# Two edge layers of a graph network: GpSimd's gathers of table rows are tied to TensorE's one-hot gathers

## The chip, the cores and the metric

The kernel runs on one core of one Trainium2 chip. The metric is the device time of that core in microseconds. The kernel before took 4427.94 us, the median of three runs that lie between 4411.06 and 4448.39 us.

## The reference

The network has 6250 nodes with 16 features and 206250 edges, sorted by their destination. Four layers follow each other, each as `x = x + layer(relu(layernorm(x)))`. The first (six graph convolutions) and the third (one) are done as dense products with an adjacency matrix. The change touches only the second and the fourth, whose messages hang on each edge's own type:

```
# second layer, 8 edge types
A     = edge_emb[edge_type_8].reshape(-1, 16, 16)
msg   = einsum('emh,eh->em', A, h[src])
m     = segment_sum(msg, dst, 6250)          # then a GRU step of m and h
# fourth layer, 90 edge types
e     = concat([h[src] @ Ws.T, edge_attr @ Ws.T, h[dst] @ Ws.T]) @ Wa.T
msg   = einsum('ei,eio->eo', h[src], W_rel[edge_type_90]) * e
h_out = segment_sum(msg, dst, 6250)
```

## The kernel before, in words

The edges are padded to 206848 and cut into 202 **supertiles** of 1024 edges (8 columns of 128 edges). Both edge layers go through the supertiles in one loop each, and each supertile is done in one of two ways.

- **By matmul** ("one-hot supertiles"). SyncE loads the source keys of the 1024 edges, VectorE compares them with `at_key` and writes one-hot matrices (`make_hot`, L1818 in the second layer, L2195 in the fourth), TensorE multiplies the node table with them (`gather`, 24 matmuls at L1832 and 4 at L1828, or 28 at L2214), ScalarE evicts the result in four pieces (L1838, L2220), TensorE folds it (L1848, L2229), and the messages are made and summed by destination. The fourth layer also expands the relation weights with 24 matmuls (L2249) and multiplies on VectorE (L2277, L2269).
- **By table.** A table of all products (node, type) was written to HBM before (`typed_table`). GpSimd fetches each edge's finished row with an indirect DMA, 8 of them for a supertile, one for 128 edges (`fetch_rows`, L1809; `fetch_table_rows`, L2180). TensorE sums the rows by destination (`row_sums`, L1915; `add_up`, L2301).

In the second layer (`typed_layer`) 122 supertiles go by matmul (list `PK`) and 80 by table (list `GK`). In the fourth (`relation_layer`) list `EK` holds 106: the first 11 are "plain" (GpSimd fetches rows of h, L2166, while TensorE still builds the table, L2133), 95 go by matmul, and 96 go by table (`GK`). `after[i]` lists the table supertiles that lie behind the i-th entry of PK or EK. It holds one or none in the second layer, and one nearly always in the fourth, where three places hold two: i = 43, 74 and 105, the last.

The loop is software-pipelined and written out by hand. Turn i issues, in this order on the engines: the key loads of a later supertile (SP), the table fetches of `after[i]` (POOL), the fold of supertile i-1 (PE, ACT), the destination one-hots and one-hots for i+1 (DVE), the gather of supertile i (PE), and the sums of older ones, among them the table supertiles of `after[i-3]` (second layer) or `after[i-2]` (fourth). Between engines only semaphores order the work. GpSimd's queue holds nothing but its fetches in these loops, so it runs ahead of the turn that issues them until it finds no free buffer: `fetch_rows(g)` waits for the sums of table supertile g-8 (`a_tok[g - RG]`, RG = 8), `fetch_table_rows(g)` for those of g-12 (RT = 12). The first fetch of each layer waits for the table's last stores. The token `gat[i, HALVES - 1]` is given by TensorE's last matmul of the gather of supertile i; ScalarE and VectorE wait for it too.

After each edge layer there is a barrier of all engines.

Of the kernel before, what the change touches and what calls it, by code (L numbers as in the profile page):

```python
# [55 lines left out]
HALVES = 2  # L56
# [64 lines left out]
def program(nc, t, wcols, out):  # L121
    pe, dve, act, pool, sp = nc.tensor, nc.vector, nc.scalar, nc.gpsimd, nc.sync
# [1156 lines left out]
    def layers_fast(h_tok):  # L1279
# [414 lines left out]
        def typed_layer(x_spread, HT):  # L1694
# [6 lines left out]
            after = [[g for g, k in enumerate(GK) if PK[i] < k and (i + 1 == n or k < PK[i + 1])] for i in range(n)]  # L1701
# [37 lines left out]
            keys_tok, hot_tok, gat, selt, fold_tok, G_tok, typed_tok, byt_tok, bytc_tok, m_tok, a_tok, dst_tok, r_tok_, sum_tok, out_tok = ({} for _ in range(15))  # L1739
# [52 lines left out]
            def load_keys(i):  # L1792
                b = i % 3
                if i >= 3:
                    sp.wait_ge(*hot_tok[i - 3])
                e = slice(PK[i] * SE, (PK[i] + 1) * SE)
                k_in[b].by(sp.dma_start(krow[b][:, :], key2_dram[:, e].to_broadcast([P, SE])), 16)
                rows8 = last_dram[2 * PK[i]:2 * PK[i] + 2].rearrange("h r e -> (h r) e").rearrange("r (q e) -> r q e", q=1)
                keys_tok[i] = k_in[b].by(sp.dma_start(klast[b][:, :], rows8.to_broadcast([8, LASTK, HE])), 16)
# [157 lines left out]
            for i in range(n + 3):  # L1957
                if i + 2 < n:
                    load_keys(i + 2)
                if i == n:  # L1960
                    sp.wait_ge(*hot_tok[n - 1])
                    sp.wait_ge(*gat[n - 1, HALVES - 1])
                    load_place(RING, passes.order[::-1][RING])
                if i < n:
                    for g in after[i]:
                        fetch_rows(g)
                if 1 <= i <= n:
                    fold_rows(i - 1)
                    keep_rows(i - 1)
                if i >= 2 and i - 2 < n:  # L1970
                    for g in after[i - 2]:
                        make_dst(g)
                if i + 1 < n:
                    make_hot(i + 1)
                if 1 <= i <= n:
                    make_typed(i - 1)
                if i < n:
                    gather(i)
                if i >= 2:
                    sum_types(i - 2)  # L1980
                if 2 <= i <= n + 1:
                    keep_types(i - 2)
                if i >= 3:
                    keep_sums(PK[i - 3], m_tok[i - 3], i - 3)
                    store_sums(PK[i - 3], i - 3)
                    for g in after[i - 3]:
                        row_sums(g)
                        keep_sums(GK[g], a_tok[g])
                        store_sums(GK[g])
# [42 lines left out]
        def relation_layer(x_spread, terms, wx, w_ready):  # L2032
# [23 lines left out]
            after = [[g for g, k in enumerate(GK) if EK[i] < k and (i + 1 == n or k < EK[i + 1])] for i in range(n)]  # L2056
            by_matmul = [kinds[k] == "matmul" for k in EK]
# [30 lines left out]
            keys_tok, hot_tok, ty_tok, gat, selt, fold_tok, G_tok, w_tok, prod_tok, e_tok, msg_tok, a_tok, sum_tok = ({} for _ in range(13))  # L2088
# [240 lines left out]
            for i in range(n + 2):  # L2329
                tiles = range(min(NT, TILES[i]), min(NT, TILES[i + 1])) if i < PLAIN else ()  # L2330
                if i + 1 < n:
                    load_edges(i + 1)
                if i < n:
                    for g in after[i]:
                        fetch_table_rows(g)
                ahead = 1 if 1 <= i < PLAIN else len(tiles)
# [176 lines left out]
```

## Time and profile before

| what | value |
|---|---|
| median of three runs | 4427.94 us (4411.06 to 4448.39) |
| profiled execution, span from first to last instruction | 4521.8 us |
| mean granted TensorE clock in it | 0.868 |
| PE busy | 3700.8 us (82%) |
| DVE busy | 2709.2 us (60%) |
| POOL busy | 1876.4 us (41%) |
| ACT busy | 1320.5 us (29%) |
| loop of the second layer | about 1478 to 2733 us of the span |
| loop of the fourth layer | about 2950 to 4504 us, by matmul and table from about 3059 us |

The profile shows one execution. For that execution no time besides its span is given, and the span is 93.9 us longer than the median of the timed runs. An engine's share counts its instructions alone, not its waits. A matmul's end is modelled in the profile, so that the moment at which another engine is released by it tells more of TensorE's real progress than the matmul rows do. "issue" as the end of idle time means that the profile shows nothing for which the engine waited; "remote" that the semaphore's giver could not be named. The granted clock is a share of 2.4 GHz: 1.00 is 2.4 GHz, 0.50 is 1.2 GHz, and other values are means over a stretch.

### The profile page before, as it was taken

The page shows a single profiled execution, that of the slowest core. Times are in us where ns is not written, and L with a number is a line of the kernel's source. Part 1 is how long each engine was busy: PE and PEld are TensorE (multiplying, and loading weights), DVE is VectorE, ACT ScalarE, POOL GpSimd, SP SyncE. Part 2 cuts the span into 40 slices and gives each one's busy share as a digit, 9 for nine tenths or more (in the row PEclk, how much of TensorE's full clock was granted, in tenths as well). Part 3 has the DMA queues.
Part 4 walks back from the last instruction along what each step waited for, and adds up shares of the span by engine and source line. Part 5 has one row for each costly group of instructions (what it writes and reads, how often), then busy time and mean ns, then how long its engine had stood idle before and what let it go on. Part 6 is the DMA issues. An engine that isn't in the chain of part 4 may idle for free. (4 is left out here: it accounts for less than half of the span.)

```text
span 4521.8 us, 77858 instructions
## 1 busy us (share of the span) xinstructions
PE 3700.8 (82%) x28548; PEld 2135.0 (47%) x28548; DVE 2709.2 (60%) x6415; ACT 1320.5 (29%) x2874; POOL 1876.4 (41%) x1856
## 2 busy tenths in 40 slices
PE   6778869999997488897888795482799988998898
PEld 4666635544554143443444443241455555555555
DVE  8999933222213265666666574252577777776778
ACT  7899910011000122332332231150122212221222
POOL 1000058400000545666666540437366565655550
PEclk8999979999997688898899897665788889888888
DMA  5444477533447111221122126671122221221111
GB/s 143 80 80 80 80 316 286 213 150 153 162 184 295 45 44 41 51 51 45 46 49 49 41 51 200 216 261 34 31 47 43 43 41 39 47 41 40 42 40 42
DMA packets 471197, 445.63 MB, mean 99 GB/s; under 512 B 357554, under 2 KB 406610, under 8 KB 459676
## 3 DMA queue, kind: packets, MB, share of 16 engines
q1 hardware_dynamic: 389178, 391.82, 27.6%
q0 software_dynamic: 55216, 38.70, 5.1%
q10 hardware_dynamic: 26417, 10.05, 0.9%
q8 instruction: 232, 3.80, 0.3%
q14 instruction: 154, 1.25, 0.1%
HBM read 346.18 MB, written 95.85 MB: 98 GB/s over the span
## 5 line engine op out<-in xcount | busy, mean ns | idle before, releaser
L1809 POOL DMA_INDIRECT rows<-typed_table,ring x640 | 734.7, 1148 | 472.0 <-PE ps_x L1915 263.5
L2214 PE MATMUL l_ps_g<-ring,h_part 128*128 128x512 f16 x2660 | 656.3, 406 | 142.8 <-issue 101.5
L1409 PE MATMUL L_ps<-ring,L_T 128*128 128x448 fp8e4 (+1 forms) x4606 | 678.3, 394 | 68.6 <-DMA ring<-adj 54.2
L2180 POOL DMA_INDIRECT ring<-typed_table,l_idxA x384 | 397.9, 1036 | 349.7 <-PE l_ps_x L2301 192.5
L1409 PEld LDWEIGHTS L_ps<-ring,L_T 128*128 128x128 f16 (+1 forms) x4606 | 329.6, 107 | 403.9 <-issue 70.0
L2214 PEld LDWEIGHTS l_ps_g<-ring,h_part 128*128 128x128 f16 x2660 | 275.0, 104 | 492.6 <-issue 202.3
L2180 POOL DMA_INDIRECT l_rows<-typed_table,l_idxA x384 | 393.8, 1025 | 248.5 <-PE l_ps_x L2301 144.0
L2220 ACT ACTIVATE l_sel<-l_ps_g 128x512 f16<-128x512 f32 x380 | 225.4, 597 | 900.6 <-PE l_ps_g L2214 373.9
L619 PE MATMUL cells<-keys,lows 128*128 128x147 f16 (+5 forms) x2744 | 373.1, 283 | 119.5 <-DVE keys L580 104.0
L1838 ACT ACTIVATE sel<-ps_g 128x512 f16<-128x512 f32 x488 | 264.1, 595 | 537.4 <-PE ps_g L1832 314.0
L2195 DVE TENSOR_SCALAR ring<-l_krow,W 128x1024 f16<-128x1024 f16 x570 | 234.7, 482 | 301.0 <-remote 164.9
L2249 PE MATMUL l_ps_w<-rel,l_tyh 90*128 90x256 bf16 x2544 | 400.1, 328 | 17.1 <-DVE ring L2277 12.1
L1832 PE MATMUL ps_g<-dinvB,h_part 128*128 128x512 f16 x1464 | 383.2, 422 | 27.9 <-issue 27.8
L619 PEld LDWEIGHTS cells<-keys,lows 128*128 128x128 f16 x2744 | 286.8, 141 | 203.1 <-DVE keys L580 170.7
L1868 DVE TENSOR_TENSOR dinvB<-G,tyh 128x1024 f16<-128x1024 f16 x244 | 288.2, 1222 | 135.3 <-issue 87.4
L1421 DVE SCALAR_TENSOR_TENSOR L_Y<-L_ps,L_scale,dinvB 128x448 f32<-128x448 f32 x84 | 57.4, 683 | 520.3 <-PE L_ps L1409 520.2
L580 DVE TENSOR_SCALAR keys<-build_or_wx,offset 128x441 f16<-128x441 f16 (+3 forms) x1438 | 366.3, 329 | 0.0
L1832 PE MATMUL ps_g<-ring_fifth,h_part 128*128 128x512 f16 x1464 | 349.8, 394 | 11.3 <-issue 10.7
L2249 PEld LDWEIGHTS l_ps_w<-rel,l_tyh 90*128 90x128 bf16 x2544 | 287.9, 116 | 99.4 <-issue 27.2
L697 ACT ACTIVATE ring<-cells 128x784 fp8e4<-128x784 f32 x392 | 325.1, 830 | 24.7 <-PE cells L619 24.4
L2277 DVE TENSOR_TENSOR ring<-l_ps_w,l_G 128x512 f32<-128x512 f32 x380 | 258.6, 683 | 85.2 <-remote 71.3
L2269 DVE TENSOR_REDUCE l_msg<-ring 128x32 f32<-128x512 f32 x424 | 277.6, 676 | 0.0
(369 smaller groups left out, 4468.1 us busy)
## 6 DMA issues: line engine op xcount, KB each, us to landing
ring<-adj SPq DMA_DIRECT2D x67, 2744.0 KB, 10.3
adj<-ring SPq DMA_DIRECT2D x14, 2744.0 KB, 9.1
typed_table<-ring SPq DMA_DIRECT2D x49, 765.0 KB
ring_fifth<-src_div_mod_rows SPq DMA_DIRECT2D x122, 256.0 KB
l_krow<-src_div_mod_rows SPq DMA_DIRECT2D x95, 256.0 KB
l_trow<-type_row SPq DMA_DIRECT2D x106, 180.0 KB
attr<-in_he POOLq DMA_DIRECT2D x25, 512.0 KB, 8.1
klast<-last_keys SPq DMA_DIRECT2D x81, 128.0 KB
```

Source lines behind the costliest of these rows:

```text
L580: ins = dve.tensor_scalar(keys[g % OB][:, j, 0:C], iotaC[:, 0:C], offset[g // BG % 2][:, g % BG, j:j + 1], HIT, ALU.is_equal, ALU.mult)
L619: ins = pe.matmul(to, lows[g // QG % 3][:, :, g % QG * KT + j], made[:, (a1 - a) * NT:(b1 - a) * NT], start=j == FIRST[h], stop=j == LAST[ ...
L697: act.activation(ring[c % RING][:, :, gl * GD:(gl + 1) * GD].rearrange("p k (h d) -> p k h d", h=2), cells[g % CB][:, :, 0:HD * NT].rearra ...
L1409: ins = pe.matmul(bank[at:at + rows, 0:CH], d["T"][q][:, k, 0:rows], ring[r][:, k, :], start=n < side, stop=n >= NT - side, tile_position= ...
L1809: r_tok_[g] = r_in[b].by(pool.indirect_dma_start(rows[b][:, j, :], None, t1_dram, bass.IndirectOffsetOnAxis(ap=idxA[:, k * SUP + j:k * SUP ...
L1832: ins = pe.matmul(ps_g[2 * h + p][:, 0:HE], parts[p][:, j, :], hot[b][:, j, h * HE:(h + 1) * HE], start=False, stop=j == GJ - 2)
L1838: selt[i, h] = c_sel.by(act.activation(sel[b][2 * h + p][:, :], ps_g[2 * h + p][:, 0:HE], ACT.Relu))
L1868: typed_tok[i] = c_typed.by(dve.tensor_tensor(typed[b][:, p, :, :, :], gp, ty, ALU.mult))
L2180: rt_tok[g] = r_in[b].by(pool.indirect_dma_start(table_rows[b][:, j, 0:RC], None, t3_dram, bass.IndirectOffsetOnAxis(ap=idxA[:, k * SUP + ...
L2214: ins = pe.matmul(ps_g[p][:, 0:HE], parts[p][:, j, :], hot[b][:, j, h * HE:(h + 1) * HE], start=j == 0, stop=j == GJ - 1)
L2249: ins = pe.matmul(ps_w[q][:, (j % 2) * 256:(j % 2 + 1) * 256], tyh[i % 3][:, j * P:(j + 1) * P], rel[:, p, :], start=p == 0, stop=p == 2)
L2269: return c_msg.by(dve.tensor_reduce(m[:, 2 * q:2 * q + 2, 0:F], prod[q], AX.X, ALU.add))
```

## The change

Before the fetches of turn i, GpSimd now waits until TensorE has finished the gather of supertile i-2, in both layers. In the fourth layer the wait is left out where supertile i-2 is a plain one. Nothing else changes: no buffer, no size, no other wait.

```
@@ -1962,6 +1962,8 @@        (typed_layer)
                     sp.wait_ge(*gat[n - 1, HALVES - 1])
                     load_place(RING, passes.order[::-1][RING])
                 if i < n:
+                    if i >= 2 and after[i]:
+                        pool.wait_ge(*gat[i - 2, HALVES - 1])
                     for g in after[i]:
                         fetch_rows(g)
                 if 1 <= i <= n:
@@ -2331,6 +2333,8 @@        (relation_layer)
                 if i + 1 < n:
                     load_edges(i + 1)
                 if i < n:
+                    if i >= 2 and after[i] and by_matmul[i - 2]:
+                        pool.wait_ge(*gat[i - 2, HALVES - 1])
                     for g in after[i]:
                         fetch_table_rows(g)
                 ahead = 1 if 1 <= i < PLAIN else len(tiles)
```

## Rows read from the trace of the kernel before

**Rows 1.** The page, engines: busy time, share of the span, instructions.
```profile
PE 3700.8 (82%) x28548; PEld 2135.0 (47%) x28548; DVE 2709.2 (60%) x6415; ACT 1320.5 (29%) x2874; POOL 1876.4 (41%) x1856
```

**Rows 2.** Windows, fourth layer, L2180 alone: us, POOL busy (count), clock, DMA, GB/s.
```profile
3059.00:3183.00 124.00, 94.10 (x96) 0.54 0.12 19
3183.00:3232.00 49.00, 0.00 (x0) 0.81 0.12 32
```

**Rows 3.** Windows, fourth layer: us, busy of PE, PEld, DVE, ACT, POOL; clock, DMA, GB/s.
```profile
3078.00:3196.00 118.00, 21.29 (x88) 6.96 (x86) 11.08 (x25) 2.01 (x5) 79.08 (x84) 0.53 0.09 11
3196.00:3232.00 36.00, 35.21 (x266) 21.45 (x266) 30.95 (x72) 9.38 (x21) 0.00 (x0) 0.87 0.16 43
...
3300.00:4300.00 1000.00, 902.20 (x7028) 554.59 (x7027) 735.90 (x1682) 211.98 (x491) 595.98 (x576) 0.87 0.21 42
...
4401.00:4490.00 89.00, 89.00 (x808) 57.58 (x805) 80.63 (x185) 24.87 (x57) 0.33 (x1) 1.00 0.11 31
```

**Rows 4.** Windows, fourth layer, L2220 alone, four evictions for each gather.
```profile
3078.00:3196.00 118.00, 1.54 (x3) 0.53 0.09 11
3196.00:3232.00 36.00, 7.90 (x14) 0.87 0.16 43
...
3300.00:4300.00 1000.00, 165.67 (x279) 0.87 0.21 42
...
4401.00:4490.00 89.00, 19.60 (x33) 1.00 0.11 31
```

**Rows 5.** Timeline of DVE in the fourth layer: start, us, instruction, idle before.
```profile
3115.89 0.69 DVE L2277 TENSOR_TENSOR ring<-l_ps_w,l_G 128x512 f32<-128x512 f32 x1 [21.62 <-remote]
...
3149.44 0.69 DVE L2277 TENSOR_TENSOR ring<-l_ps_w,l_G 128x512 f32<-128x512 f32 x1 [31.51 <-remote]
```

**Rows 6.** Timeline of PE in the second layer, while GpSimd gathers.
```profile
1550.99 0.58 PE L1832 MATMUL ps_g<-dinvB,h_part 128*128 128x512 f16 x1 [2.21 <-issue]
1553.79 0.58 PE L1832 MATMUL ps_g<-dinvB,h_part 128*128 128x512 f16 x1 [2.21 <-issue]
```

**Rows 7.** Windows, second layer, L1809 alone (columns as in rows 2).
```profile
1479.00:1563.00 84.00, 64.19 (x64) 0.62 0.11 21
1563.00:1605.00 42.00, 0.00 (x0) 0.87 0.15 39
...
1700.00:2660.00 960.00, 604.90 (x520) 0.89 0.21 47
```

**Rows 8.** Windows, second layer, L1838 alone, four evictions for each gather.
```profile
1485.00:1526.00 41.00, 4.56 (x9) 0.71 0.10 16
1526.00:1575.00 49.00, 2.28 (x5) 0.51 0.05 5
1575.00:1605.00 30.00, 9.29 (x18) 1.00 0.21 55
...
1700.00:2660.00 960.00, 209.99 (x388) 0.89 0.21 47
...
2677.00:2721.00 44.00, 12.92 (x25) 1.00 0.15 40
```

**Rows 9.** Timeline of DVE, second layer, one-hots of two turns running.
```profile
1582.09 2.46 DVE L1818 TENSOR_SCALAR ring_fifth<-ring_fifth,W 128x1024 f16<-128x1024 f16 x6 [1.49 <-PE ps_g L1832]
...
1589.44 2.46 DVE L1818 TENSOR_SCALAR dinvB<-ring_fifth,W 128x1024 f16<-128x1024 f16 x6 [0.89 <-PE ps_g L1832]
```

**Rows 10.** Timeline, fourth layer: last eviction of gather 23, first use of group 12.
```profile
3343.58 0.60 ACT L2220 ACTIVATE l_sel<-l_ps_g 128x512 f16<-128x512 f32 x1 [0.86 <-remote]
...
3381.19 0.29 DVE L2293 TENSOR_TENSOR ring<-ring,l_eG 128x128 f32<-128x128 f32 x1
```

**Rows 11.** Timeline, end of the second layer: evictions of gather 119, last row sums.
```profile
2706.04 1.08 ACT L1838 ACTIVATE sel<-ps_g 128x512 f16<-128x512 f32 x2 [1.50 <-PE ps_g L1832]
...
2727.98 1.04 PE L1915 MATMUL ps_x<-rows,dstw 128*64 128x16 f32 x16 [0.36 <-ACT sums L1926]
```

More of the change, by code:

```diff
@@ L1964, in typed_layer @@
                 if i < n:
+                    if i >= 2 and after[i]:
+                        pool.wait_ge(*gat[i - 2, HALVES - 1])
                     for g in after[i]:
@@ L2333, in relation_layer @@
                 if i < n:
+                    if i >= 2 and after[i] and by_matmul[i - 2]:
+                        pool.wait_ge(*gat[i - 2, HALVES - 1])
                     for g in after[i]:
```

## The prediction

> **What bounds the kernel now.** I read the engines' shares first. TensorE is busy 82% of the span, GpSimd 41% [rows 1], so no gather of GpSimd's should be on the path by its share. Then I laid windows over the two loops that the change touches, and beside each asked for GpSimd's gathers alone and for ScalarE's evictions alone. Four evictions make one TensorE gather, so their count is the speed at which the loop goes.
>
> In the fourth layer GpSimd may start once the table is stored. It then runs through all its twelve free buffers: 96 gathers in 124 us, and then it stands still for 49 us [rows 2]. Over the same time TensorE nearly stops. From 3078 to 3196 us there are 3 evictions, less than one gather, and the granted clock is 0.53; when the burst is over, 36 us see 14 evictions, 3.5 gathers, at 10.3 us each [rows 3, 4]. The steady part, where GpSimd gathers one group per turn, takes 1000 us for 279 evictions: 14.3 us a gather at a clock of 0.87. The last 89 us have no gather of GpSimd's, and 33 evictions: 10.8 us each at a clock of 1.00, with the same work on every other engine [rows 3, 4].
>
> The stall is TensorE's own. VectorE waits 21.6 and 31.5 us for the products of twelve matmuls each [rows 5]; the two releases are 33.6 us apart, 2.8 us for each matmul. In the second layer the matmul rows show that pace directly, one each 2.80 us with "issue" before it, so no semaphore of the profile holds it [rows 6]. There the burst is 64 gathers in 84 us [rows 7]; its gathers 1 to 3 take from 1485 to 1575 us (14 evictions, window edges included) and then 4.5 gathers take 30 us, where the one-hots of two turns start 7.35 us apart [rows 8, 9]. With GpSimd busy it is 960 us for 388 evictions, 9.90 us a gather; in the last 44 us without it, 25 evictions, 7.0 us [rows 8].
>
> So the profile says: while GpSimd gathers, TensorE is slower by 14.3 - 10.8 = 3.5 us a turn in the fourth layer and by 9.9 - 7.35 = 2.5 us in the second, and after some 20 us of unbroken gathering it falls to a crawl. Slower gathering with pauses costs TensorE far less than a burst.
>
> **The change, part by part.** The added waits are some 170 on a queue that holds nothing else in these loops; behind each stands only the group that it guards. Their own time is at most an ordinary step of that queue: the burst's 96 gathers take 1.28 us each with 0.98 us of it busy [rows 2], so 0 to 0.3 us, hidden, since GpSimd has idle time in every turn (596 us busy in 1000 [rows 3]).
>
> *The bursts go.* In the fourth layer groups 0 and 1 still start early (the first has no wait, the second one for gather 11, which is done before 3078), but group 2 waits for gather 12, group 3 for gather 13, and so on. The pace of the steady part should hold from there. From 3078 to 4490 us, 94 gathers take 1412 us now (the ends of the windows of [rows 4]). At 14.34 us (1000 x 4 / 279) they take 1348 us: **-64 us**. This already charges the ten groups that used to be fetched in the stall, and the end of the loop, now without gathers, at the full steady price.
>
> In the second layer the first group (behind entry 4 of PK) waits for gather 2. Gathers 1 and 2 then go at 7.35 us: 14.7 us instead of 41 (1485 to 1526 [rows 8]). The 119 gathers from 3 to 121 take 119 x 9.90 = 1178 us, instead of 1195 (1526 to 2721): together **-43 us**.
>
> The other way round: the stalls are worth 118 - 14.3 = 104 us and 90 - 22 = 68 us (three gathers at 7.35), and the gathers that move to where TensorE now runs alone cost, per turn, 3.5 us for 8.25 turns (29), 14.3 - 10.3 = 4 us for 3.5 turns (14), 9.9 - 7.0 = 2.9 us for 6.25 turns (18) and 9.9 - 6.7 = 3.2 us for 4.5 turns (14) [rows 4, 8]: 172 - 75 = 97 us. The two sums agree within 10 us. I take 107, since it uses the long steady windows.
>
> *Arrival of the rows.* A group was fetched up to twelve groups ahead and now starts when gather i-2 is done. In the fourth layer gather 23 is done at 3343.6 and the rows of turn 25 are first used at 3381.2 [rows 10], 37.6 us later. A group of eight takes 8 x 1.28 = 10.3 us, and two together, where `after` holds two, 20.6. That is hidden, with 17 us to spare. If that cover went, each such place would cost a few us, three times. The tightest place is the end of the second layer: group 79 may start at 2706.0, but groups 77 and 78 are before it (gates 14.7 and 7.35 us earlier, 8 x (604.9 / 520 + 0.3) = 11.7 us each), so it ends near 2691.3 + 3 x 11.7 = 2726.4, and TensorE wants it at 2728 [rows 7, 9, 11]. I set 0 us and keep 0 to 5 us for the range.
>
> *Where two rows and a rule differ.* Rows 3 and 6 show TensorE slow only while GpSimd gathers. That is also the sign that this is contention and not a wait. The Trainium skill (SBUF — State Buffer, section "Who interferes with whom") states the contrary: a DMA never contends with a compute engine, only VectorE and GpSimd share ports, and TensorE and ScalarE never wait on anyone. By that rule the bursts could not be what stalls TensorE, and the change would bring nothing from them.
>
> Sum: -107 us on a span of 4521.8, that is 4415. The timed median stands 94 us below that span, and I carry the difference over unscaled: 4427.9 - 107 = **4321 us**. What part of the slowdown is there without the profiler is the main unknown. Its bounds are 0 and all. The slowdown beside gathers that the windows hold is 172 us of stalls, 1000 / 14.3 x 3.5 = 245 us and 960 / 9.9 x 2.5 = 242 us [rows 4, 8], 659 us together. The timed runs are only 94 us shorter than the span, so most of it must be in them too. I stay near "all".
>
> **The rivals.** *Half.* TensorE starts to crawl soon after 3078 us, when GpSimd has gathered for only 19 us, and groups 0 and 1 (22 us) and the pairs of the second layer remain unbroken. If half of the stalls stays, 172 / 2 - 75 = 11 us are won: 4417.
>
> *Only in the profile.* The 94 us between span and runs are of the size of the stalls that would go. If the crawl belongs to the profiled execution, the timed runs don't change: about 4428. Against it speak the 659 us above. The Trainium skill (NOTIFIC — the notification-queue block, section 7.1) says that the path of the trace records can hold an engine back; no row here shows that path.
>
> *Slower.* The stall is not due to the burst but to the start of the loop (first keys, cold buffers), and happens anyway at the same place; then only the price of moved gathers is left, +75 us: 4503. It decides against the change from the point where less than 75 of the 172 us go away. For it: gathering and TensorE's work overlap more than before. Against it: the crawl ends 12 or 13 us after the burst in both layers (3183 and 3196, 1563 and 1575 [rows 2, 4, 7, 8]), at different places of their loops, and VectorE and ScalarE only wait in it. The rule above would favour this case or the one before.
>
> **How the numbers follow.** Forecast 0.60, half 0.10, only in the profile 0.17, slower 0.13. The forecast's own range is 4270 to 4375: lower if the steady part of the fourth layer becomes quicker too (0.5 us a turn makes 47), higher if a third of the stalls stays (+57). The range to 4440 takes in the rivals "half" and "only in the profile" and leaves out the slower one and the forecast's lower tail. 1% (44 us) is about what a measurement of this kernel can tell from no change. Faster by more: 0.61; within: 0.26; slower: 0.13.
>
> **What would show it.** In the changed kernel's profile: no window of 100 us with fewer than 20 evictions at L2220 or L1838; GpSimd's 96 and 64 gathers spread out, its idle time ended by the gather's matmuls (L2214, L1832) instead of the sums (L2301, L1915); a steady turn of 14.3 and 9.9 us in the whole loop, and the clock no longer 1.00 in the last 90 us; no wait of VectorE's for fetched rows before L2292, none of TensorE's before L1915. The prediction is wrong if the two stalls stay, if a steady turn becomes longer than 15 or 10.5 us, or if the span falls and the runs don't.

## The result

| | median of the runs | ratio to before |
|---|---|---|
| before | 4434.97 us (4411.06 to 4448.39, 4 runs) | |
| changed | 4517.26 us (4512.33 to 4557.44, 4 runs) | 1.0203 [1.0155, 1.0252] |

The ratios, here and below, leave disturbed runs out, so they aren't always those of the medians. The forecast was 4321 us and faster. The kernel is 2% slower, and the time lies outside the range. The profiled execution of the changed kernel is one of its timed runs: 4512.33 us, with a span of 4508.4 us. Against the profiled execution of before (span 4521.8 us) it is 13 us *shorter*, so the two traces by themselves don't show the loss. Why is part of the answer below.

The page, engines, to lay beside [rows 1]:

```profile
PE 3746.4 (83%) x28548; PEld 2133.2 (47%) x28548; DVE 2704.2 (60%) x6415; ACT 1319.3 (29%) x2874; POOL 1915.0 (42%) x1856
```

The same instructions, and TensorE is busy 46 us longer. The windows of GpSimd's gathers at the start of the fourth layer, which now begins near 3104 us (the line numbers there have moved by two, L2180 is L2182; columns as in [rows 2]):

```profile
3104.00:3228.00 124.00, 70.89 (x65) 0.88 0.24 48
3228.00:3277.00 49.00, 34.28 (x32) 0.90 0.28 49
```

The 96 gathers in 124 us have become 65, and the 49 us of standing still are gone. Now the evictions of the one-hot gathers in the fourth layer, L2222, four for each gather, the answer to [rows 4]:

```profile
3123.00:3241.00 118.00, 21.39 (x36) 0.93 0.24 45
3241.00:3277.00 36.00, 5.37 (x9) 0.86 0.30 49
3345.00:4345.00 1000.00, 163.28 (x276) 0.86 0.22 41
4387.00:4476.00 89.00, 13.62 (x23) 0.83 0.13 19
```

The first 118 us hold 36 evictions where there were 3, and the clock in them is 0.93, not 0.53: the stall is gone. The steady part has 276 instead of 279 evictions in 1000 us. The last 89 us hold 23 instead of 33, because GpSimd now gathers to the end. The second layer, L1838, the answer to [rows 8]:

```profile
1481.00:1522.00 41.00, 9.45 (x18) 0.92 0.12 24
1522.00:1571.00 49.00, 8.68 (x16) 0.82 0.20 46
...
1700.00:2660.00 960.00, 195.09 (x364) 0.84 0.20 44
2730.00:2775.00 45.00, 7.67 (x15) 0.77 0.12 24
```

Here too the stall at the start is gone (34 evictions in 90 us, before 14). But the steady part has slowed: 364 evictions in 960 us are 10.55 us a gather, before it was 388 and 9.90 us, and the clock has gone from 0.89 to 0.84. What released GpSimd (sum of the waits, times, longest), of the whole span:

```profile
POOL rows L1809 <- PE ps_g L1832: 375.5, 37, 31.0
POOL ring L2182 <- PE l_ps_g L2216: 196.8, 29, 60.5
...
POOL l_rows L2182 <- PE l_ps_g L2216: 119.2, 27, 13.2
```

So the change does what it says: TensorE's gathers of the one-hot tiles release GpSimd in both layers. Two of the prediction's own signs of being wrong came true: a steady turn of the second layer is longer than 10.5 us, and the span fell while the runs didn't.

### The profile page after: what moved, and what is told of

It reads as the page before. It is cut to its first block and busy times, and to the rows that moved or that the text cites. A ratio compares the mean times of both kernels' runs of the same rounds, so it can differ in the third digit from the quotient of the medians.

```text
span 4508.4 us, 78017 instructions
## 1 busy us (share of the span) xinstructions
PE 3746.4 (83%) x28548; PEld 2133.2 (47%) x28548; DVE 2704.2 (60%) x6415; ACT 1319.3 (29%) x2874; POOL 1915.0 (42%) x1856
## 5 line engine op out<-in xcount | busy, mean ns | idle before, releaser
L1809 POOL DMA_INDIRECT rows<-typed_table,ring x640 | 731.3, 1143 | 564.3 <-PE ps_g L1832 375.5
L2182 POOL DMA_INDIRECT ring<-typed_table,l_idxA x384 | 419.1, 1091 | 317.8 <-PE l_ps_g L2216 196.8
L2182 POOL DMA_INDIRECT l_rows<-typed_table,l_idxA x384 | 415.6, 1082 | 242.7 <-PE l_ps_g L2216 119.2
L1838 ACT ACTIVATE sel<-ps_g 128x512 f16<-128x512 f32 x488 | 262.5, 596 | 561.7 <-PE ps_g L1832 347.2
L2222 ACT ACTIVATE l_sel<-l_ps_g 128x512 f16<-128x512 f32 x380 | 224.9, 597 | 644.2 <-PE l_ps_g L2216 415.1
L1832 PE MATMUL ps_g<-ring_fifth,h_part 128*128 128x512 f16 x1464 | 400.5, 439 | 2.6 <-issue 2.2
L2251 PEld LDWEIGHTS l_ps_w<-rel,l_tyh 90*128 90x128 bf16 x2544 | 269.2, 111 | 169.4 <-issue 111.4
```

The costliest lines, as they stand in the source:

```text
L1809: r_tok_[g] = r_in[b].by(pool.indirect_dma_start(rows[b][:, j, :], None, t1_dram, bass.IndirectOffsetOnAxis(ap=idxA[:, k * SUP + j:k * SUP ...
L1832: ins = pe.matmul(ps_g[2 * h + p][:, 0:HE], parts[p][:, j, :], hot[b][:, j, h * HE:(h + 1) * HE], start=False, stop=j == GJ - 2)
L1838: selt[i, h] = c_sel.by(act.activation(sel[b][2 * h + p][:, :], ps_g[2 * h + p][:, 0:HE], ACT.Relu))
L2182: rt_tok[g] = r_in[b].by(pool.indirect_dma_start(table_rows[b][:, j, 0:RC], None, t3_dram, bass.IndirectOffsetOnAxis(ap=idxA[:, k * SUP + ...
L2251: ins = pe.matmul(ps_w[q][:, (j % 2) * 256:(j % 2 + 1) * 256], tyh[i % 3][:, j * P:(j + 1) * P], rel[:, p, :], start=p == 0, stop=p == 2)
```

## Experiments

Ten different kernels, the kernel before among them, ran 18 times under a name of their own in five sittings, each beside runs of the kernel before on the same chip. The kernel before itself took very different times in them: 4530 us in sitting A, 3792 in B, 4511 in C, 4442 in D and 4449 in E. A, C and D were one chip, B and E two others. "Slowed" below means that TensorE is slower while GpSimd gathers, as in the trace ahead of the prediction; that was so in A, C, D and E and not in B.

### Sitting A (before 4530 us): each layer's wait alone

`b0_before` is the kernel before, unchanged. `typed_only` and `relation_only` are one half of the change each:

```
typed_only      +  if i >= 2 and after[i]:                          (second layer)
                +      pool.wait_ge(*gat[i - 2, HALVES - 1])
relation_only   +  if i >= 2 and after[i] and by_matmul[i - 2]:     (fourth layer)
                +      pool.wait_ge(*gat[i - 2, HALVES - 1])
lag6            both, with i - 6 in place of i - 2
```

> The kernel before, unchanged, for a second trace of it. Theory 'the profiled execution was not a typical one': the timed runs of before (median 4435) are some 90 us shorter than the one traced, and 90 us is about what the stalls at the start of the two loops cost, so the new trace has a span near 4430 and at least one of the stalls (119 us before gather 12 of the fourth layer, 49 us before gather 3 of the second) is gone or much shorter. Theory 'the stalls are always there': the span is again near 4520 or, if it is 4430, the steady turns are shorter and the two stalls stand. Ratio to before 1.00.

Measured: 4532.71 us, ratio 1.0036 [0.9997, 1.0074].

> The wait in the second layer alone. In the changed kernel's trace a turn of that loop takes 10.7 us against 9.9 in the trace of before, with GpSimd's groups in unbroken pairs. Theory 'pairs': the slow-down of the second layer is the larger part of the 82 us, so this kernel takes 50 to 80 us more than before (4485 to 4515). Theory 'moved gathers': each layer pays for the groups that used to be fetched in a burst, 8 here and 10 to 11 there, so this kernel takes 30 to 40 us more than before (4465 to 4475).

Measured: 4545.0 us, ratio 1.0046 [0.9997, 1.0095].

> The wait in the fourth layer alone. Theory 'pairs' (most of the loss is in the second layer): 5 to 30 us more than before (4440 to 4465). Theory 'moved gathers': 40 to 50 us more (4475 to 4485). If the stall before gather 12 were in the typical run of before, this kernel would be 60 us faster.

Measured: 4450.39 us, ratio 0.987 [0.9789, 0.995].

> Both waits, but for gather i-6 instead of i-2 (in the fourth layer the wait then begins at turn 17, so that four groups run free). The burst is limited to about 4 groups, and GpSimd stays some 7 turns ahead instead of 3. Theory 'moved gathers': the loss goes with the number of groups that no longer come early, so about half of the 82 us remains: 4470 to 4480. Theory 'pairs' (it is the moment in the turn and the unbroken pair that count, and both are as with i-2): nearly the whole loss remains, 4500 to 4520.

Measured: 4597.6 us, ratio 1.0166 [1.0074, 1.0257].

What follows: the stalls are no peculiarity of the one execution that was given, since `b0_before` shows them too and its span (4553.6 us) is 4 us below its own time. The fourth layer's wait wins there, by the mechanism of the prediction and near its size: its loop is 70 us shorter than in `b0_before` (the forecast's term was 64). Both theories that were written down for `relation_only`, 5 to 30 and 40 to 50 us more than before, missed. The second layer's wait wins nothing, although it too takes its stall away. And waiting on an older gather (i - 6), which leaves GpSimd a lead of six turns, is not the cure: the second loop got longest of all, 1361.5 us.

### Sitting B (before 3792 us): a chip on which TensorE isn't slowed

`after_again` is the changed kernel. `slots4` caps the burst of the second layer in another way, by row sums and not by gathers; its fourth layer is that of before. `halves` splits a group's eight fetches over two turns. `half_gathers` is the kernel before with half of the second layer's fetches left out, so that half of these messages is missing; it also clears the row buffers once (not shown).

```
slots4        -  if g >= RG:                       +  if g >= 4:
              -      pool.wait_ge(*a_tok[g - RG])  +      pool.wait_ge(*a_tok[g - 4])
halves        -  for j in range(SUP):
              +  for j in range(half * SUP // 2, (half + 1) * SUP // 2):
              (fetch_rows(g, 0) after gather i-3, fetch_rows(g, 1) after gather i-2)
half_gathers  -  for j in range(SUP):              +  for j in range(SUP // 2):
```

> The changed kernel, unchanged, beside before on the chip of this job. In the traces so far the wait in the fourth layer shortens its loop from 1404-1428 to 1355-1362 us, and the wait in the second layer moves its loop from 1211-1252 to 1247-1294 us. Theory 'two opposite effects, and a chip-dependent remainder': the sum is near zero, ratio to before 0.99 to 1.01. Theory 'the loss is the change's own everywhere': ratio 1.015 to 1.025 again.

Measured: 3865.84 us, ratio 1.0193 [1.017, 1.0216].

> The kernel before, but in the second layer a group may only be fetched when the sums of group g-4, not g-8, are done; the fourth layer as before. So the start burst is 4 groups, and GpSimd is about as near to TensorE as with the added wait, but it is released at the row sums, as before, and not at the end of the gather. Theory 'amount' (what counts is how many groups run ahead): like the wait in the second layer alone, loop 1247 to 1294 us, turns of 10.4 to 10.7. Theory 'moment' (what counts is at which point of TensorE's turn a group begins): turns of 9.5 to 9.9 as before, loop 1200 to 1220 us, 20 to 40 us less than before.

Measured: 3805.88 us, ratio 1.0029 [1.0014, 1.0045].

> The changed kernel, but in the second layer a group is fetched in two halves of four gathers: the first after gather i-3, the second after gather i-2. Two neighbouring groups then make runs of 4, 8 and 4 gathers in three turns instead of one run of 16. Theory 'length of the run' (TensorE slows in the later part of an unbroken run): turns of 9.0 to 9.6 in the second layer instead of 10.7, 100 us or more less than the changed kernel. Theory 'sum of the gathers' (each gather costs TensorE the same, wherever it runs): 10.4 to 10.8 us a turn as in the changed kernel.

Measured: 3857.28 us, ratio 1.0167 [1.0134, 1.02].

> The kernel before, with only 4 of the 8 gathers of each group in the second layer (the other four columns of rows hold zeros, so half of these messages is left out). The work of TensorE, VectorE and ScalarE is the same. Theory 'sum of the gathers': a turn takes the mean of 7.35 (no gathers) and 9.8 (all), 8.5 to 8.7 us. Theory 'length of the run': runs of 5.2 us are too short to slow TensorE, so 7.4 to 7.8 us; the start burst of 32 gathers (42 us) makes a stall of less than half of the 49 to 66 us seen.

Measured: 3739.05 us, ratio 0.9863 [0.9843, 0.9882].

The same 2% as in the first comparison, but it must have another cause: on this chip there is no stall that could be won. The start and the steady part of the fourth layer in `slots4`, whose fourth layer is that of before, GpSimd's gathers (L2180) first and the evictions (L2220) after:

```profile
2720.00:2845.00 125.00, 98.48 (x88) 0.96 0.28 56
2900.00:3500.00 600.00, 467.47 (x435) 1.00 0.29 55
```

```profile
2720.00:2845.00 125.00, 26.28 (x44) 0.96 0.28 56
2900.00:3500.00 600.00, 130.80 (x219) 1.00 0.29 55
3500.00:3740.00 240.00, 51.96 (x87) 1.00 0.29 53
```

88 fetches run in 125 us, 44 evictions beside them, and after it 219 in 600 us: 10.96 us a gather at full clock, with GpSimd never idle but for its steps of 0.30 us. `after_again`, its gathers (L2182) and then its evictions (L2222):

```profile
2900.00:3500.00 600.00, 471.70 (x422) 0.99 0.28 52
```

```profile
2900.00:3500.00 600.00, 125.49 (x211) 0.99 0.28 52
3500.00:3740.00 240.00, 49.14 (x83) 1.00 0.26 51
```

11.4 and 11.6 us a gather. What VectorE waits for in `after_again` from 3200 us on (total, times, longest):

```profile
DVE l_eG L2294 <- DMA l_rows<-typed_table,l_idxA: 42.0, 27, 8.8
DVE l_eG L2294 <- DMA ring<-typed_table,l_idxA: 37.9, 25, 8.7
```

In `slots4` the same row is one wait of 6.3 us. So TensorE's loop waits for fetched rows, and GpSimd has become the bound. One group costs 8 x (1.12 + 0.30) = 11.4 us there (the mean gather of the fourth layer and the step between two), and a turn without any hindrance is 10.95 us. GpSimd loses some 0.45 us a turn, 42 us in the 94 turns, and has no lead to spend on it.

The lost lead is only part of that, for the fetches themselves have become dearer: the same eight take 11.06 us in `slots4` and 11.40 in `after_again` (first to last fetch, over 96 groups). At 11.06 us the loss would be 0.1 us a turn, an estimate of 10 us for the whole loop. The dearer ones sit at one place: the fourth of the eight takes 1.79 us on the mean in `after_again` and 0.98 in `slots4`. The fetches beside which VectorE writes the type one-hots (L2202, in `slots4` L2200) take 2.06 us on the mean against 0.99 for all others, in `slots4` 1.68 against 0.99. So the wait ties the fetches to a place of the turn here too; that VectorE's work there is what lengthens them was not tested.

The fourth loop is 1070.0 instead of 1027.7 us and what follows it 47.0 instead of 38.7 us. That is 51 of the 73 us; the second layer's loop (957.3 us, in `slots4` 945.4) gives 12 more against `slots4`, which is itself 13 us behind before.

`half_gathers` bears the bound out: with four fetches a group every turn of the second layer takes 7.35 us (loop 889.3 us), so what holds its loop above 889 us on this chip is GpSimd: in `slots4` 608 of the 640 fetches form one stretch without a pause, at 12.2 us a group. `halves` gives no answer to its own question, the length of a run of fetches, since there too 636 of the 640 form one stretch; it is 0.2% below `after_again`, with a second loop of 949.4 us.

### Sitting C (before 4511 us): once more, and a wait with a lead

`relation_again` and `typed_again` are the halves once more, `lag6_again` is `lag6`, and `relation_lag6` has the wait of the fourth layer alone, on gather i-6:

```
relation_lag6   +  if i >= 6 and after[i] and by_matmul[i - 6]:     (fourth layer)
                +      pool.wait_ge(*gat[i - 6, HALVES - 1])
```

> The wait on gather i-2 in the fourth layer alone, once more, since it gave a ratio of 0.987 on one chip where TensorE is slowed beside GpSimd's gathers (13 to 14.5 us a turn). Theory (a burst stalls TensorE, and the wait takes away GpSimd's lead): which sign wins depends on whether TensorE is slowed. Where the loop's steady turn is 10.95 us, its pace without GpSimd, there is no stall to win; GpSimd's group of eight (11.4 to 11.8 us) is longer than the turn and its lead is gone, so the loop from gather 11 to 105 takes 1070 us instead of 1028 and the end 47 us instead of 39: +50 us, ratio 1.013. Where the steady turn is 13.5 us or more: no stall at the start, -60 to -80 us, ratio 0.983 to 0.988. Rival (the wait costs a fixed amount wherever it runs): ratio 1.01 in both.

Measured: 4432.25 us, ratio 0.9811 [0.9745, 0.9877].

> The wait on gather i-2 in the second layer alone, once more. Theory: where turns without GpSimd's slowing are 7.35 us the eight fetches of a group take longer than the turn (12 us for two of three turns, 8 a turn on the mean), so taking the lead of eight groups away puts some of the wait for rows on TensorE: +10 to +25 us, ratio 1.003 to 1.007, and the fourth layer stays at 1028 us. Where TensorE is slowed: the start's stall goes (-40 us) and the steady turn rises from 9.8 to 10.4 us or more (+60 us): +15 us, ratio 1.004. Rival (the whole of the changed kernel's +2% lies in this layer): ratio 1.015 or more.

Measured: 4514.56 us, ratio 0.9996 [0.9957, 1.0035].

> The wait in the fourth layer alone, but on gather i-6, so that GpSimd may be up to some seven groups ahead and cannot fetch all twelve buffers in one go. Theory: the lead of some seven turns hides the 0.5 to 0.8 us by which a group is longer than a turn of 10.95 us, so where TensorE isn't slowed it costs nothing (ratio 0.998 to 1.002, loop 1028 us, end 38 us, no 25 us turn after the two groups of i = 74); where TensorE is slowed the burst is seven groups instead of twelve, with more room between: -40 to -70 us, ratio 0.985 to 0.991. Rival (any wait on TensorE's gathers costs as the one on i-2 does, by the wait itself or by keeping GpSimd beside TensorE): as relation_again, ratio 1.013.

Measured: 4470.64 us, ratio 0.9854 [0.9772, 0.9936].

> Both layers wait on gather i-6. On the chip where TensorE is slowed this gave 1.0166, nearly all of it in the second layer (loop 1361 us instead of 1252, turns of 11.4 us). Theory of the lost lead: where TensorE is not slowed, a lead of six turns hides GpSimd, both loops are as before (second 945 us, fourth 1028 us), ratio 0.998 to 1.003, and what it cost elsewhere is only more of the slowing. Rival (the wait in the second layer has a price of its own, whatever the lead): second loop 1000 us or more, ratio above 1.01.

Measured: 4583.86 us, ratio 1.0145 [1.0084, 1.0207].

TensorE was slowed again, so these repeat A rather than test the lead on the chip of B, which stays untested. The gain in the fourth layer is real (-1.9%, -1.5% with the older gather). Waiting on the older gather in the second layer costs again: its loop takes 1331.8 us although GpSimd keeps six turns of lead. On such a chip it is not the lost lead that makes the second layer slow.

### Sitting D (before 4442 us): the two waits side by side

`both_third` is the changed kernel, `relation_third` the fourth layer's wait alone, `before_traced` the kernel before, and `relation_slots4` is `relation_third` with the cap of `slots4` in the second layer:

```
relation_slots4 -  if g >= RG:                                      (second layer)
                -      pool.wait_ge(*a_tok[g - RG])
                +  if g >= 4:
                +      pool.wait_ge(*a_tok[g - 4])
                +  if i >= 2 and after[i] and by_matmul[i - 2]:     (fourth layer)
                +      pool.wait_ge(*gat[i - 2, HALVES - 1])
```

> The changed kernel, beside the wait of the fourth layer alone on the same chip. Where TensorE is slowed beside the gathers (before near 4520 us), two theories. A: the two waits act alone and add up: 1.000 to 1.005 times 0.981 to 0.987, so 0.985 to 0.99, and the +2% of the changed kernel needs another ground. B: on the chip of the first comparison (before 4435 us) TensorE was slowed less, and the changed kernel takes the same 4510 us everywhere that it is slowed: ratio 0.995 to 1.0 here. Rival C: the second layer's wait costs more once the fourth has one too: ratio 1.01 or more, second loop 1290 us as in the changed kernel's first trace. Where TensorE is not slowed (before near 3790 us): 1.019 again.

Measured: 4518.31 us, ratio 1.019 [1.007, 1.031].

> The wait in the fourth layer alone. Where TensorE is slowed (turns of 13.5 us or more): 0.981 to 0.987 again. Where it is not: ratio 1.013 (+50 us), the fourth loop 1070 us instead of 1028 and the end 47 instead of 39 us, since GpSimd's group (11.4 to 11.8 us) is longer than the turn of 10.95 us and has no lead. Rival (the second layer's wait makes the whole difference there): 1.00.

Measured: 4410.78 us, ratio 0.996 [0.991, 1.0009].

> The wait on gather i-2 in the fourth layer, and in the second none on gathers, but the fetch of group g waits for the sums of g-4 instead of g-8. Where TensorE is slowed: the second layer's first burst is four groups instead of eight, and GpSimd still starts when row sums are done and not when a gather is done. Theory (the phase matters: a start at the end of a gather lays the fetches beside the many small matmuls that follow): second loop 10 to 40 us shorter than in relation_third, ratio 0.972 to 0.982. Rival (any tighter hold lengthens the steady turn): second loop 20 us longer or more, ratio 0.987 or more. Where TensorE is not slowed: 1.013 as relation_third, plus 0.003.

Measured: 4375.22 us, ratio 0.9845 [0.9794, 0.9896].

> The kernel before, for a trace on the same chip: ratio 1.00. Where TensorE is slowed: first gather of the fourth layer by matmul followed by a stall of some 110 us, second loop 1235 to 1252 us, fourth 1413 to 1428 us. Where it is not: no stall in either burst, second loop 935 to 950 us, fourth 1028 us, end 38 us. Rival for the latter (the changed kernel's longer fourth loop there has nothing to do with the wait): fourth loop 1060 us or more in this trace.

Measured: 4443.69 us, ratio 0.9975 [0.9919, 1.003].

This is the first comparison over again: before at 4442, changed +1.9%. With the fourth layer's wait alone nothing is lost, so the loss lies in the second. My expectation for `relation_third` (0.981 to 0.987) missed: the wait gave a time like those of A and C (4411 against 4450 and 4432 us), but the kernel before was 70 to 90 us quicker. For the same reason `before_traced` missed its loops (1180.1 and 1375.0 us, expected 1235 to 1252 and 1413 to 1428). `relation_slots4` missed narrowly: 0.9845 where 0.972 to 0.982 was expected, though its second loop is 52 us shorter than that of `relation_third` (10 to 40 expected). It is better than both kernels, and shows that it matters on what GpSimd waits. Its evictions in the second layer (L1838), then those of `both_third`:

```profile
1490.00:1570.00 80.00, 17.26 (x32) 0.84 0.14 33
1700.00:2600.00 900.00, 204.58 (x380) 0.90 0.23 49
```

```profile
1490.00:1570.00 80.00, 17.77 (x34) 0.89 0.16 35
1700.00:2600.00 900.00, 184.65 (x344) 0.85 0.20 45
```

And those of `before_traced`:

```profile
1490.00:1570.00 80.00, 4.34 (x8) 0.57 0.08 8
1700.00:2600.00 900.00, 207.17 (x384) 0.89 0.23 49
```

Both ways take the stall away (32 and 34 evictions in 80 us, before 8). Held by row sums, the steady part stays as it was (380 against 384 in 900 us). Held by the gathers, it loses 10% (344), at a clock of 0.85 instead of 0.89 or 0.90.

### Sitting E (before 4449 us): the second layer's wait where before is quick

`typed_third` is the second layer's wait alone, `both_fourth` the changed kernel.

```
typed_third     +  if i >= 2 and after[i]:                          (second layer)
                +      pool.wait_ge(*gat[i - 2, HALVES - 1])
```

> The wait in the second layer alone, for the first time in one sitting with the changed kernel. In the last sitting (before 4442 us) the changed kernel stood at 1.019 and the fourth layer's wait alone at 0.996, so the second layer's wait must be worth some +2.3% beside the other; by itself it gave 1.0046 and 0.9996 in sittings with before near 4520 us. Theory S (it hangs on the sitting: where before is near 4440 us its second loop holds 1180 us, and the wait stretches it to 1250 to 1280 us): ratio 1.015 to 1.025 here if before is near 4440 us, 1.000 to 1.005 if it is near 4520 us. Theory I (the two waits act on each other, whatever the sitting): 1.000 to 1.005 in either. Where TensorE isn't slowed (before near 3790 us): 1.003 to 1.007.

Measured: 4547.66 us, ratio 1.0231 [1.0187, 1.0275].

> The changed kernel. Theory S: if before is near 4440 us 1.019 to 1.021 again, if it is near 4520 us 0.985 to 1.00, since the second layer's wait then costs next to nothing. Theory I: 1.015 or more in either, second loop 1277 to 1294 us and 30 us or more above that of typed_third, though both have the same instructions there. Where TensorE isn't slowed: 1.019.

Measured: 4531.77 us, ratio 1.0171 [1.0123, 1.0219].

Theory S holds and theory I falls: the second layer's wait costs 2.3% by itself where before takes some 4445 us. And the waits add up: 1.0231 x 0.996 (from D) is 1.019, and the changed kernel gave 1.019 and 1.0171.

## Where the time went

The loops of all traces in which TensorE is slowed, worked out from the start of ScalarE's last eviction of each gather. The second loop runs from gather 0 to gather 121; "start" is its first four turns, "turn" the mean of the other 117. The fourth runs from gather 11 to gather 105; "start" is its first turn, "turn" the mean of the other 93. All in us.

| kernel | second loop | start | turn | fourth loop | start | turn |
|---|---|---|---|---|---|---|
| before (given) | 1235.3 | 96.6 | 9.73 | 1413.0 | 119.0 | 13.91 |
| b0_before (A) | 1252.4 | 102.3 | 9.83 | 1428.0 | 122.0 | 14.04 |
| before_traced (D) | 1180.1 | 97.7 | 9.25 | 1375.0 | 110.7 | 13.59 |
| relation_only (A) | 1211.3 | 96.6 | 9.53 | 1358.0 | 18.8 | 14.40 |
| relation_again (C) | 1210.9 | 96.2 | 9.53 | 1340.1 | 11.0 | 14.29 |
| relation_third (D) | 1196.7 | 102.3 | 9.35 | 1347.2 | 16.0 | 14.31 |
| relation_lag6 (C) | 1221.5 | 102.3 | 9.57 | 1369.7 | 46.9 | 14.22 |
| typed_only (A) | 1247.4 | 39.5 | 10.32 | 1404.3 | 119.4 | 13.82 |
| typed_again (C) | 1220.3 | 39.4 | 10.09 | 1426.5 | 118.5 | 14.06 |
| typed_third (E) | 1267.0 | 39.0 | 10.50 | 1383.9 | 110.1 | 13.70 |
| changed (result) | 1294.1 | 39.2 | 10.73 | 1354.6 | 12.3 | 14.43 |
| both_third (D) | 1277.2 | 38.9 | 10.58 | 1316.3 | 15.3 | 13.99 |
| both_fourth (E) | 1310.7 | 39.0 | 10.87 | 1352.2 | 17.1 | 14.36 |
| lag6 (A) | 1361.5 | 49.2 | 11.22 | 1361.7 | 46.7 | 14.14 |
| lag6_again (C) | 1331.8 | 45.7 | 10.99 | 1356.5 | 46.5 | 14.09 |
| relation_slots4 (D) | 1144.7 | 49.2 | 9.36 | 1358.4 | 18.8 | 14.41 |

Down the columns:

- **Fourth layer, wait on i-2**: the start falls from 117 us (mean of six traces) to 16 (of seven), -101 us. The turn rises from 13.85 to 14.31 us, 93 x 0.46 = +43 us. Together **-58 us**.
- **Second layer, wait on i-2**: the start falls from 99 us (seven traces) to 39 (six), -60 us. The turn rises from 9.54 to 10.52 us, 117 x 0.97 = +114 us. Together **+54 us**.

On the mean the two cancel. That is also what the two given traces say, 4521.8 against 4508.4 us. But the kernel before isn't the same from one sitting to the next: 4530 and 4511 us in A and C, 4435 to 4449 us in the first comparison, D and E. The kernels with the second layer's wait hardly follow it: 4545, 4515 and 4548 us (`typed_*`), 4517, 4518 and 4532 us (both waits). Where before is quick, they are 2% behind. The changed kernel itself was never timed in a sitting where before is slow, so that it would draw level there is inferred from its parts. In D the three spans add up: `both_third` 4467.2 against `before_traced` 4424.8 us, +42.4 us, of which the second loop is +97.1, the fourth -58.7 and everything else +4.0. (This execution of `both_third` was its quickest, 4471 us; its median is 4518.)

**Why the turn gets longer in the second layer** is shown only in part. Not by waiting for rows: TensorE's waits in that loop of the changed kernel name ScalarE or nothing. Total, times, longest:

```profile
PE ps_x L1848 <- ACT sel L1838: 99.3, 65, 2.9
PE ps_x L1880 <- issue: 56.5, 116, 2.6
PE ps_x L1915 <- issue: 32.0, 65, 1.7
```

It is TensorE that is slowed, now in the small matmuls between two large gathers. The timeline of PE in `both_third` (start, us, instruction, idle before), while GpSimd fetches two groups in one go from 1899.6 to 1922.5 us:

```profile
1899.82 0.67 PE L1915 MATMUL ps_x<-rows,dstw 128*64 128x16 f32 x15
...
1907.24 0.26 PE L1880 MATMUL ps_x<-dsth,dinvB 128*128 128x64 f16 x3 [0.44 <-issue]
1907.95 0.31 PE L1880 MATMUL ps_x<-dsth,dinvB 128*128 128x64 f16 x5 [0.45 <-issue]
1908.68 0.28 PE L1880 MATMUL ps_x<-dsth,dinvB 128*128 128x64 f16 x4 [0.42 <-issue]
...
1911.56 0.56 PE L1848 MATMUL ps_x<-fold,sel 128*128 128x16 f16 x16 [2.38 <-ACT sel L1838]
...
1921.23 0.32 PE L1915 MATMUL ps_x<-rows,dstw 128*64 128x16 f32 x5 [0.44 <-issue]
```

Unhindered, the 16 matmuls of L1880 are one row of 0.63 us. Here three to five come every 0.7 us, with "issue" before them, and the fold behind them waits 2.38 us more, for ScalarE. ScalarE itself had waited for TensorE (`both_third`, same stretch):

```profile
1902.57 0.18 ACT L1926 ACTIVATE dinvB<-ps_x 128x16 f32<-128x16 f32 x1 [1.79 <-remote]
1905.85 0.38 ACT L1855 ACTIVATE G<-ps_x 128x256 f16<-128x256 f32 x1 [3.10 <-remote]
1909.44 2.06 ACT L1838 ACTIVATE sel<-ps_g 128x512 f16<-128x512 f32 x4 [3.21 <-remote]
```

Here the profile names no giver; by the program the three waits are for TensorE's row sums, fold and next gather. ScalarE gets the row sums at 1902.57 and the fold at 1905.85 us, though the rows of PE let these matmuls end at 1900.49 and 1901.07. What is slow are thus the row sums and the fold, right behind the large gather whose end released GpSimd; the rows of L1880, before which the "issue" stands, begin before ScalarE gets the next gather at all. The rows of PE show the slowing too late, and the releases are the better measure. GpSimd's fetch that starts this stretch is released by the end of a one-hot gather (`both_third`, the first row below). In `before_traced` a fetch like it is released by the row sums, among the last of the small matmuls (second fence):

```profile
1899.61 1.23 POOL L1809 DMA_INDIRECT rows<-typed_table,ring  x1 [9.01 <-PE ps_g L1832]
```

```profile
1919.51 1.27 POOL L1809 DMA_INDIRECT rows<-typed_table,ring  x1 [4.83 <-PE ps_x L1915]
```

I cut each turn in two by ScalarE's releases, over 100 turns (gathers 10 to 109): from a gather's last matmul to its folded rows (L1838's third eviction to L1855), where all small matmuls lie, and from there to the next gather's last matmul.

| second layer, us a turn | small matmuls | next gather |
|---|---|---|
| `slots4`, `half_gathers` (B) | 2.05, 1.74 | 5.78, 5.61 |
| `before_traced` (D) | 3.99 | 5.40 |
| all eight held by row sums | 3.98 to 4.35 | 5.17 to 5.79 |
| `both_third` (D) | 4.91 | 5.65 |
| all six held by gather i-2 | 4.75 to 4.93 | 5.14 to 6.07 |
| `lag6`, `lag6_again` | 5.45, 5.48 | 5.90, 5.80 |

So on the slowing chips the large matmuls of the steady part go about as fast as in B, and it is the small ones that are slowed, by some 2.4 us a turn before and 3.1 us with the wait, against the 1.74 us of `half_gathers`: 0.92 of the 1.18 us between `before_traced` and `both_third` are theirs. By the rows of PE, from one matmul's start to the next one's, L1880 takes 72 to 108 us in the three traces of before, 104 to 136 us with the wait on gather i-2 and 224 and 214 us with i-6.

The length of an unbroken run of fetches is not the reason: in `lag6` 70 of the 80 groups are fetched one by one and its turn is the longest, in `relation_slots4` 64 of the 80 lie in runs of two groups or more, and its turn is 9.36 us. That the fetches' place in the turn is what matters agrees with all second loops (held by gathers: 10.09 to 11.22 us, with a lead or without; held by sums: 9.25 to 9.83 us, with eight groups or with four). Why it matters is not settled; only these two places of the turn were tried. Nor is it settled what differs between the sittings.

## Why the prediction failed

- **The bursts stall TensorE**: right where it is slowed. 117 becomes 16 us and 99 becomes 39 us, a gain of 101 and 60 us; the prediction had 104 and 68. The rule set against it (the Trainium skill, SBUF — State Buffer, section "Who interferes with whom") has it that DMAs and TensorE don't hinder each other. In sittings A, C, D and E the traces disagree: 8 evictions in 80 us beside the burst, 32 when it is capped (D). On the chip of B it agrees: 44 evictions in 125 us beside 88 fetches. So the stall was there on two chips and not on a third, which ran in one sitting; one trace can't tell that.
- **"The pace of the steady part should hold from there"**: in the fourth layer nearly, -58 us against the -64 predicted. In the second layer this is the step that failed: "The 119 gathers from 3 to 121 take 119 x 9.90". They took 10.73 a turn, and the term of -43 us became +54 us on the mean, and +59 us between the two given traces. In the terms of the prediction's other sum, the price of the moved gathers in the fourth layer was right (29 + 14 = 43 us, measured 43), and that of the second was too low (18 + 14 = 32 us, measured 114). I took the price of a gather of GpSimd's from windows in which row sums set its start, and used it for a kernel that starts them elsewhere in the turn.
- **Two sums that agreed**: the other sum (172 - 75 = 97 us) came from the same windows and the same assumption, and so could not find it.
- **"I carry the difference over unscaled"**: this is the other half of the miss. Of 4517.3 - 4321 = 196 us, 98 are this step: the 94 us by which the profiled execution of before lay above the timed median were no cost of being profiled. The changed kernel's runs are 4 us above their spans, and so are those of before in A and D. The 94 us are of the size by which the kernel before differs between sittings (4442 and 4530 us on one chip), and with the second layer's wait the quicker time no longer comes. That the given trace was taken in such another sitting is argued, not shown. The rest: second loop +102 us (predicted 1192, 1294.1), fourth +6 (1349, 1354.6), outside of them -14, and +5 from the profiled run to the median: 98 + 102 + 6 - 14 + 5 = 197.
- **Arrival of the rows, 0 us**: right where TensorE is slowed, since no wait for rows shows. It failed on the chip of B, by 51 us in the fourth layer. "17 us to spare" was the slack of one turn; the question that was missing is how long a group is beside an unhindered turn. The rows had 10.3 us [rows 2] against 10.8 [rows 4], next to no margin; on the chip of B it is 11.4 against 10.95 with the wait (11.06 without it). There it is most of the loss.
- **The rivals**: "slower" gave 4503 us, near the time measured, but by luck: its reason was that the stalls stay, and they went. What it charged for moved gathers (75 us) is of the right kind and too small: the changed kernel pays 43 + 114 us for its steady turns. "Only in the profile" is refuted by the timed gains of the fourth layer's wait, and "half" by the starts of the loops.

## A version that beats both

`relation_slots4`: the fourth layer waits on gather i-2, the second layer holds GpSimd to four groups by their row sums. 4375 us in sitting D, 0.9845 [0.9794, 0.9896] of before and 3% below the changed kernel there. It was not run on the chip of B. The parts measured there (`slots4` +0.3%, and +51 us from the fourth layer's wait in `after_again`) speak for an estimate of 1.6% slower on a chip that doesn't slow TensorE; `relation_lag6`, with its lead of six turns, may be the safer choice for the fourth layer (0.9854 in C), but was not run in B either.

## What to carry to other kernels

Capping a burst and setting where in the turn each transfer starts are two changes: a wait does both, so ask what used to release the queue in the steady state and whether the new release lies at a worse place. Before a lead is taken away, compare the producer's time for one unit, at the place of the turn where it will now run, with the consumer's unhindered turn, and not with the turn that a slowed engine shows. And where the profiled execution and the timed runs of a kernel differ by more than a few us, ask whether they come from different sittings before one is corrected by the other.

## What the runs showed of the chips

- The same kernel takes 3792 us on one chip and 4442 to 4530 us on another, 17 to 19% more; instructions and data are the same. Nearly all of the difference lies where GpSimd gathers: beside them turns of 7.83 and 10.94 us in `slots4` on the quick chip, against 9.25 and 13.59 in `before_traced`; the slow one comes down to some 7 and 10.8 us only in the last turns, when the gathers are over [rows 4, 8]. Between `before_traced` (4424.8 us) and `slots4` (3802.1 us) the second loop differs by 235 us, the fourth by 347 us, the stretch between them, which has gathers too, by 44 us, and all the rest by -3 us.
- On one and the same chip the kernel before took 4530, 4511 and 4442 us in three sittings.
- The granted clock falls where TensorE is slowed, a mix of the levels 1.2 and 2.4 GHz: 0.57 in the second layer's burst (80 us of `before_traced`), 0.84 and 0.89 where the burst is capped by sums or by gathers. On the chip of B it is 0.96 in the fourth layer's burst and 1.00 behind it, beside the same gathers.
- One indirect fetch of 128 rows costs GpSimd 0.94 us at least, 1.03 to 1.2 us on the mean of a loop, and 0.30 us before the next. The mean goes with the place of the turn: 1.08 us in `slots4` and 1.12 in `after_again`, in the fourth layer on one chip.
- TensorE isn't slowed evenly beside the fetches: in the second layer's steady part the stretch of small matmuls takes 4.0 to 5.5 us a turn instead of 1.7 to 2.1, that of the large ones 5.1 to 6.1 us as in B (5.6 to 5.8).
